# Two-layer state-space and gated-scan network with routed experts: step-width products moved from VectorE to GpSimd, and the second router's rows turned back by TensorE instead of rebuilt by GpSimd

## What is computed

```python
# layer 0, attention part: a selective state-space model, 256 inner channels, 16 states
dt = softplus(einsum('blr,dr->bld', dt, W_dt) + b_dt)        # the step width
A_bar = exp(dt[..., None] * A)
Bu = dt[..., None] * Bm[:, :, None, :] * xc[..., None]       # step width * input * B
_, h_all = associative_scan(comb, (A_bar, Bu), axis=1)
y = einsum('bldn,bln->bld', h_all, Cm) + D_param * xc
...
# layer 1, expert part: h is the modulated layer norm, routed to 2 of 16 experts
h = _layernorm(x, axis=-1) * (1 + cb) + sb
x = x + gb * _L1_ffn_ref(h, ...)                             # scores from h, experts on h
```

## Time and profile before

| what | value |
|---|---|
| runs without profile, median of 3 | 703.18 us (699.43 to 703.41) |
| the profiled execution, span | 766.7 us; no other time of it is recorded |
| VectorE (DVE) busy | 503.8 us (66%) |
| GpSimd (POOL) busy | 438.7 us (57%) |
| TensorE (PE) busy | 525.1 us (68%), mean granted clock 0.816 |
| ScalarE (ACT) busy | 334.2 us (44%) |
| state-space stage, first bu to last GpSimd product | 48.90 to 303.94, 255.0 us |

### The profile page before, as it was taken

One profiled execution on the slowest core, in us unless ns is written; L12 is line 12 of the kernel. 1 busy time (PEld: TensorE's weight loads), 2 busy tenths in 40 slices (PEclk: granted clock), 3 DMA queues, 4 the chain that ended last, 5 costly groups with the idle time before them and its releaser, 6 DMA issues.

```text
span 766.7 us, 8988 instructions
## 1 busy us (share of the span) xinstructions
PE 525.1 (68%) x2044; PEld 326.2 (43%) x2045; DVE 503.8 (66%) x909; ACT 334.2 (44%) x644; POOL 438.7 (57%) x331
## 2 busy tenths in 40 slices
PE   4568949987998889456767791678147777566630
PEld 2223314423433334356657791236125555355530
DVE  5958898899799899741422244448852667754526
ACT  3265834645575453112222245646013777970004
POOL 0047968986898998145655644307236663067650
PEclk9878979997998799657987896668557999799775
DMA  5043424332323420125656764000101112211115
GB/s 170 0 154 97 125 101 154 123 125 73 107 100 109 135 86 22 37 84 147 186 156 180 192 180 124 0 0 17 39 18 45 41 38 24 110 41 44 38 45 160
DMA packets 45292, 69.56 MB, mean 91 GB/s; under 512 B 6146, under 2 KB 25188, under 8 KB 45124
## 3 DMA queue, kind: packets, MB, share of 16 engines
q1 hardware_dynamic: 39684, 57.69, 24.3%
q0 software_dynamic: 5568, 11.41, 5.6%
HBM read 59.97 MB, written 9.11 MB: 90 GB/s over the span
## 4 chain that ended last, share of the span: by engine, by line
PE 47%; DVE 17%; issue 12%; ACT 7%; another core or an unknown queue 6%; DMA 4%; POOL 3%; DVEq 2%; SPq 1%; ACTq 0%; POOLq 0%
PE ps L1021 11%; PE ps L1144 5%; PE ps L1133 4%; PE ps L988 4%; PE ps L1293 4%; DVE hs L1575 4%; PE ps L1015 3%; PE ps L1257 2%; PE ps L1183 2%; PE ps L1282 2%; POOL bu L474 2%; PE ps L958 1%; DVEq L1644 1%; PE ps L1262 1%
## 5 line engine op out<-in xcount | busy, mean ns | idle before, releaser
L474 POOL TENSOR_TENSOR bu<-uT,b_sb 128x1024 f32<-128x1024 f32 x64 | 149.5, 2356 | 29.7 <-DVE uT L1555 29.7
L444 POOL DMA_INDIRECT y_dram<-ys,rows_i x87 | 89.6, 1030 | 93.1 <-DVE ys L1832 39.5
L438 POOL DMA_INDIRECT xl<-h_dram,rows_i x87 | 90.4, 1039 | 75.6 <-DVE rows_i L1478 41.7
L1021 PE MATMUL ps<-prod,cst 128*128 128x512 f32 x256 | 129.7, 651 | 2.9 <-DVE yT L1595 2.9
L647 ACT ACTIVATE ps<-dtT,neg_a 128x512 f32<-128x512 f32 x128 | 85.6, 685 | 64.1 <-DVE hs L1575 63.6
L485 POOL TENSOR_TENSOR prod<-hs,c_sb 128x1024 f32<-128x1024 f32 x32 | 75.6, 2363 | 31.7 <-DVE hs L1575 17.6
L1021 PEld LDWEIGHTS ps<-prod,cst 128*128 128x128 f32 x256 | 50.1, 206 | 82.1 <-issue 77.6
L1575 DVE TENSOR_TENSOR_SCAN hs<-ps,carry,bu 128x512 f32<-128x512 f32 x64 | 77.6, 1265 | 5.1 <-ACT ps L647 5.1
L1575 DVE TENSOR_TENSOR_SCAN hs<-ps,bu 128x512 f32<-128x512 f32 x64 | 73.8, 1205 | 4.6 <-ACT ps L647 4.5
L1144 PE MATMUL ps<-w_s,ht 128*128 x312 | 50.2, 312 | 27.3 <-ACT ht L737 14.4
L737 ACT ACTIVATE ht<-ps,b1T 128x128 f32<-128x128 f32 x78 | 24.8, 365 | 86.8 <-remote 40.3
(11 more groups left out here) (252 smaller groups left out, 940.3 us busy)
## 6 DMA issues: line engine op xcount, KB each, us to landing
b_sb<-b_rows SPq DMA_DIRECT2D x32, 512.0 KB, 4.5
w1r<-in_w SPq DMA_DIRECT2D x39, 256.0 KB
c_sb<-b_rows SPq DMA_DIRECT2D x32, 256.0 KB, 3.6
mf_s<-in_mf SPq DMA_DIRECT2D x16, 256.0 KB
w_s<-in_w SPq DMA_DIRECT2D x9, 256.0 KB, 4.0
h_dram<-h_tok SPq DMA_DIRECT2D x8, 256.0 KB
phase_s<-in_phase SPq DMA_DIRECT2D x16, 128.0 KB
down_s<-in_down SPq DMA_DIRECT2D x1, 2048.0 KB, 7.3
```

What stands on the lines that cost most here:

```text
L438: pool.indirect_dma_start(xl[:, j % slots, :], None, h_dram[l], bass.IndirectOffsetOnAxis(ap=rows_i[:, 0, j:j + 1], axis=0)).then_inc(load ...
L444: pool.indirect_dma_start(y_dram[l], bass.IndirectOffsetOnAxis(ap=rows_i[:, 1, j:j + 1], axis=0), ys[:, j % XR, :], None).then_inc(saved[j ...
L474: nc.gpsimd.tensor_tensor(bu[:, g % RING, :, :], uT[:, c % 2, :, :], b_sb[:, k % BRING, g % 2, :].unsqueeze(1).broadcast_to([P, ND, CHUNK] ...
L1021: last = nc.tensor.matmul(bank(Y_BANK + d), ident, prod[:, g % RING, d, :], start=n == 0, stop=n == NS - 1)
```

## The change

1. In the state-space stage VectorE keeps the sum of the step width, which now counts up a new semaphore dt_sum. The product uT stays on VectorE for chunk 0 only; for chunks 1 to 3 GpSimd makes it in `step_inputs`, two instructions of 128x512 behind products(2k-1) of the last pair of the chunk before. dt_ready is now for GpSimd's `inputs` alone; all others wait for dt_sum.
2. In the second layer GpSimd's four `router_rows` are gone. TensorE turns hT back (`turn_home`, 4 transposes a chunk into PSUM bank HOME), and ScalarE copies the block into h_tok (`rows_home`, 128x512) and counts up rows1.

```diff
+HOME = PG
...
-            def router_rows(l, c, turned, count, done):
+            def router_rows(c):
...
+            def step_inputs(c, d):
+
+                q = c % 2
+                pool.wait_ge(S["dt_sum"], 2 * c + d + 1)
+                nc.gpsimd.tensor_tensor(uT[:, q, d, :], dtT[:, q, d, :], xcT[:, q, d, :], ALU.mult).then_inc(S["dt_ready"], 1)
+
             for k in range(PAIRS):
                 inputs(2 * k)
                 inputs(2 * k + 1)
                 if k:
                     products(2 * k - 1)
+                if k % (NS // 2) == NS // 2 - 1 and k + 1 < PAIRS:
+                    for d in range(ND):
+                        step_inputs(k // (NS // 2) + 1, d)
...
             inverse_std(1, "ln2", "rs2")
-            router_rows(1, 0, "t2_ps", 1, "rows1")
             inverse_std(2, "ln2", "rs2")
             inverse_std(3, "ln2", "rs2")
-            router_rows(1, 1, "t2_ps", 2, "rows1")
-            router_rows(1, 2, "t2_ps", 3, "rows1")
-            router_rows(1, 3, "t2_ps", 4, "rows1")
...
+            def rows_home(c):
+
+                act.wait_ge(S["home_ps"], c + 1)
+                nc.scalar.activation(h_tok[:, c * CT:(c + 1) * CT, :].rearrange("p t c -> p (t c)"), bank(HOME), ACT.Copy).then_inc(S["rows1"], 1)
...
             columns_router(1)
+            rows_home(0)
             normed_out(2)
             columns_router(2)
+            rows_home(1)
             normed_out(3)
             columns_router(3)
+            rows_home(2)
+            rows_home(3)
...
+            def turn_home(c):
+
+                pe.wait_ge(S["hT2"], c + 1)
+                if c:
+                    pe.wait_ge(S["rows1"], c)
+                h = chunk_of(hT, c)
+                for t in range(CT):
+                    last = nc.tensor.transpose(ps[:, HOME, t * P:(t + 1) * P], h[:, t * P:(t + 1) * P], ident)
+                last.then_inc(S["home_ps"], 1)
...
                 dve.wait_ge(S["softp_done"], 2 * c + d + 1)
-                then(nc.vector.tensor_tensor(dtT[:, q, d, :], dtT[:, q, d, :], bank(dt_bank(d)), ALU.add))
-                nc.vector.tensor_tensor(uT[:, q, d, :], dtT[:, q, d, :], xcT[:, q, d, :], ALU.mult).then_inc(S["dt_ready"], 1)
+                nc.vector.tensor_tensor(dtT[:, q, d, :], dtT[:, q, d, :], bank(dt_bank(d)), ALU.add).then_inc(S["dt_sum"], 1)
+                if c == 0:
+                    dve.wait_ge(S["dt_sum"], d + 1)
+                    nc.vector.tensor_tensor(uT[:, q, d, :], dtT[:, q, d, :], xcT[:, q, d, :], ALU.mult).then_inc(S["dt_ready"], 1)
```

More of the change, by code:

```diff
@@ L304, in adaln_two_layers @@
  "consts_b ln_stats ln_rstd h_ready hT_ps hT_sb conv_ps z_ps xc_ready zs_ready dbl_ps dtlow_sb "
- "dt_ps dt_taken softp_done dt_ready bcf_ready b_rows_saved z_raw xc_raw c_ps a_ready bu_ready scan_done prod_ready prod_pool "
+ "dt_ps dt_taken softp_done dt_sum dt_ready bcf_ready b_rows_saved z_raw xc_raw c_ps a_ready bu_ready scan_done prod_ready prod_pool "
  "sum_done y_ready o_ps x_added logit_ps logit_sb neg_ready pad_zeroed "
@@ L487, in products @@
                                         ALU.mult).then_inc(S["prod_pool"], 1)
-            def router_rows(l, c, turned, count, done):
+            def router_rows(c):
                 h = h_tok[:, c * CT:(c + 1) * CT, :]
-                wide = lambda k: mod[:, l, c // 2, k, :].unsqueeze(1).broadcast_to([P, CT, C])
-                pool.wait_ge(S[turned], count)
+                wide = lambda k: mod[:, 0, c // 2, k, :].unsqueeze(1).broadcast_to([P, CT, C])
+                pool.wait_ge(S["hT_ps"], NCHUNK + c + 1)
                 then(nc.gpsimd.tensor_tensor(h, h, wide(CB), ALU.mult))
-                nc.gpsimd.tensor_tensor(h, h, wide(SB), ALU.add).then_inc(S[done], 1)
+                nc.gpsimd.tensor_tensor(h, h, wide(SB), ALU.add).then_inc(S["h_ready"], 1)
+            def step_inputs(c, d):
+                q = c % 2
+                pool.wait_ge(S["dt_sum"], 2 * c + d + 1)
+                nc.gpsimd.tensor_tensor(uT[:, q, d, :], dtT[:, q, d, :], xcT[:, q, d, :], ALU.mult).then_inc(S["dt_ready"], 1)
             for k in range(PAIRS):
@@ L501, in _ @@
                     products(2 * k - 1)
+                if k % (NS // 2) == NS // 2 - 1 and k + 1 < PAIRS:
+                    for d in range(ND):
+                        step_inputs(k // (NS // 2) + 1, d)
             products(STEPS - 1)
-            router_rows(0, NCHUNK - 1, "hT_ps", 2 * NCHUNK, "h_ready")
+            router_rows(NCHUNK - 1)
             rows_known(0)
@@ L628, in dt_parts @@
                 if c:
-                    act.wait_ge(S["dt_ready"], 2 * c)
+                    act.wait_ge(S["dt_sum"], 2 * c)
                 nc.scalar.activation(dtT[:, c % 2, d, :], bank(b), ACT.Relu, bias=b_dt[:, d:d + 1])
@@ L642, in decays @@
                 if n == 0:
-                    act.wait_ge(S["dt_ready"], 2 * c + 2)
+                    act.wait_ge(S["dt_sum"], 2 * c + 2)
                 for d in range(ND):
@@ L972, in z_half @@
                 if d == 0 or c == 0:
-                    pe.wait_ge(S["dt_ready"], 2 * c + d + 1)
+                    pe.wait_ge(S["dt_sum"], 2 * c + d + 1)
                 else:
@@ L1030, in project_out @@
                 if c + 1 < NCHUNK:
-                    pe.wait_ge(S["dt_ready"], 2 * c + 4)
+                    pe.wait_ge(S["dt_sum"], 2 * c + 4)
                 if c and c + 1 < NCHUNK:
@@ L1043, in rows_back @@
                 if c + 2 < NCHUNK:
-                    pe.wait_ge(S["dt_ready"], 2 * c + 6)
+                    pe.wait_ge(S["dt_sum"], 2 * c + 6)
                 if c + 1 == NCHUNK:
@@ L1233, in _ @@
             rows_router(1)
+            turn_home(0)
             score_second(1)
             rows_router(2)
+            turn_home(1)
             score_second(2)
             rows_router(3)
+            turn_home(2)
             score_second(3)
+            turn_home(3)
             ranks(1, E1)
```

## The result

The changed kernel takes 707.26 us (median of 20 executions, 703.59 to 711.55) against 703.40 us for the kernel before on the same chip (20 executions): ratio 1.0049, 95% interval 1.0031 to 1.0067. The forecast was 688.3 us and the range 680 to 700, so it lies outside. On a second chip the same pair gave 1.001 (0.9981 to 1.0038). A ratio leaves out executions more than 1.5% above the fastest of their kernel; a median is over all of them.

What follows compares the result with a forecast made beforehand. GpSimd was taken to set the state-space stage's pace, with VectorE's chain bounding the second router. The stage's -9.7 us and the router's -5.2 us made -14.9 us, so 703.2 became 688.3 us; range 680 to 700 us.

Steps and rivals of the forecast that it cites:

- The 6.48 and 6.73 us of idle GpSimd go: State-space stage, ends of chunks 0 and 1: GpSimd's idle time behind VectorE's two locked-out uT products disappears, -13.2 us.
- the tiny operations: State-space stage: small VectorE operations such as the 128x4 one get in beside GpSimd each time, 1.07 us at most; nothing charged.
- Six products on GpSimd: State-space stage: six 128x512 uT products added on GpSimd at 1.27 us each, all charged, +7.6 us.
- The stretches: State-space stage: two GpSimd instructions lengthened by 0.44 us each beside VectorE's uT no longer are, -0.9 us.
- Idle time that thins out: State-space stage: a third of the remaining 14.1 us of GpSimd's idle time goes, -4.7 us.
- Router rows that get in at the next boundary: VectorE's step 15, chunks 1 and 2: each waits some 0.7 us for a running GpSimd instruction to end, +1.5 us.
- Rival 2: Lockouts multiply: three at 6.6 us each, over router rows and ln_nmr products, give 706.6 us, slower; chance 0.06.
- Second router: Second layer's router: without GpSimd's row operations VectorE is no longer blocked, so its chain shortens, -5.2 us.
- The stage forecast: The state-space stage of the changed kernel would take near 245 us, against 255.0 in the first profile.
- what would show it: Expected signs: six GpSimd uT of about 1.27 us, no long idle there, stage near 245 us, second router's mask_b earlier.
- the first sign of being wrong: State-space stage: a VectorE operation with two SBUF inputs taking over 5 us would show the prediction wrong.
- rival 3: GpSimd bounds the stage and removed idle time returns at another wait, 705.6 us; or lockouts belong to one execution; chance 0.12.

Runs made afterwards that it cites:

- before_again: The kernel before, unchanged, run again for a second profile: 743.32 us, ratio 1.0012 of the kernel before on the same chip.
- after_ln_pointer: The changed kernel with VectorE's 128x4 product ln_nmr written as four 128x1 products with a per-partition scalar: 737.27 us, ratio 0.9863 of the kernel before.
- no_two_input: Kernel before plus the second-router change, uT read from PSUM, ln_nmr by per-partition scalar, VectorE's router rows of chunks 0 to 2 left out: 732.70 us, ratio 0.9706.
- part 2 alone: The kernel before with only the second-router change, uT staying on VectorE: 738.20 us, ratio 0.9933 of the kernel before.
- before_third: The kernel before, unchanged, one execution run for a third profile: 708.83 us.
- before_fourth: The kernel before, unchanged, one execution run for a fourth profile: 757.11 us.

## Why the prediction was wrong, point by point

The step that failed is "The 6.48 and 6.73 us of idle GpSimd go (-13.2)". It took two lockouts of one profiled execution as part of the kernel's time. Four profiles of the kernel before have 2, 0, 1 and 0 lockouts, with stages of 255.0, 240.6, 247.3 and 242.1 us: each is worth some 6 to 7 us of the stage. The second failure is a term put at nothing, the tiny operations: the changed kernel has a lockout of its own, on ln_nmr, +9.3 us. The terms of the sum, with before_again as the kernel before, the changed kernel, and after_ln_pointer as the changed kernel without its lockout:

- Six products on GpSimd, +7.6: measured 7.5. Right, though the bound "between 7.6 and 8.1" contradicts its own reason: six halves of 1.18 us are 7.1.
- Two lockouts, -13.2: nothing in an execution without them. Wrong.
- The stretches, -0.9: GpSimd's product groups fall from 76.6 to 75.2 us busy, -1.4 (bu stays at 150.8). About right.
- Idle time that thins out, -4.7: it falls from 15.1 to 6.8, -8.3. Undersized: without the wait behind the convolutions (4.1 and 4.4 us) it falls from 11.0 to 2.4, more than three quarters, and I charged a third.
- Router rows that get in at the next boundary, +1.5: right in kind. The sum behind the product at step 15 takes 2.72 us in both chunks (0.69 before), 4.1 us more on VectorE. GpSimd runs on meanwhile; what the stage pays for it is in the idle time above, and no run separates it.
- "Tiny operations such as the 128x4 one got in each time": wrong. ln_nmr was held for 8.45, 8.46 and 8.48 us in all three profiles that have part 1 as it stands, +9.3 with what follows. Rival 2 had this mechanism and gave 706.6 us. That this is close to the measured time is luck: it needed three lockouts, and one was enough, since the 13.2 us weren't there to be gained.
- Second router, -5.2: measured -0.67% alone (-0.31 to -1.03), 15.0 us to mask_b where 15.2 were forecast. Right.

Without lockouts on either side the stage goes from 240.6 to 238.3 us, since 7.5 - 1.4 - 8.3 = -2.2. With the lockout of ln_nmr it is 247.4, 6.8 us more than 240.6, where the forecast had 9.7 less. So the change is -2.3 + 9.1 - 5.2 = +1.6 us against an execution of before without a lockout; measured were 3.9 and 0.7 us. The times alone don't say how many timed executions of before carry one, and some 2 us stay open.

The stage forecast ("near 245") and most signs in "what would show it" came out nearly as written, against the wrong start: a profile 14 us too long in just the stage that was changed. But the first sign of being wrong came too, a two-SBUF-input operation of over 5 us (ln_nmr, 8.45 us). I had the doubt in rival 3 ("the lockouts belong to the profiled execution alone", 63.5 us longer than the median) and gave it 0.12 together with another case, with no sum of its own. The sentence on the Trainium skill (SBUF — State Buffer, "Who interferes with whom") deserved more weight too. Its rule, that the second to issue waits until the first finishes, came to +3.5 us for the stage, with the second router -1.7 us in all. That is nearer to the measured 3.9 and 0.7 than the forecast, though it has no lockouts, and without lockouts the stage measured -2.3. It describes what most such instructions do: in the state-space stages of the 16 profiles other than no_two_input, ln_nmr in the pointer form aside, 128 VectorE instructions with two SBUF inputs were issued into a running GpSimd instruction, and 114 got in at its end. The other 14 were held over three or four more, which the rule doesn't cover.

## What to carry to other kernels

A rare, long wait in a single profile is not a term of the sum until a second profile of the same kernel shows it; where it would pay for the whole change, work out the sum without it first. Where VectorE and GpSimd both run full, find all VectorE instructions with two SBUF tensors, the tiny ones too: in several of these kernels, moving or rewriting one left another to be held. In the changed kernel, rewriting one of 128x4 so that it reads one tensor and a per-partition scalar was worth 1.5% (0.9863 against 1.001), more than the change under study; beside part 2 alone no such gain shows.

## What the runs showed of the hardware

- A VectorE instruction with two SBUF inputs, once it has lost a boundary, waited until GpSimd ran out of work: 7.70 to 10.25 us in all 14 cases, whether it works on 128x512 or 128x4. The six of 128x512 ended 0.55 us behind GpSimd's last instruction, the eight of 128x4 0.02 us behind it. Nothing came out between 2.8 and 7.7 us.
- Where the request falls matters. At a boundary from a bu to a product that followed without a pause 13 of 51 requests were held; at the other boundaries without a pause 1 of 50 (the 10.25 us one, between two bu). The last 27 of the 128 asked ahead of a pause and got in there.
- The distance from the request to the end of the running GpSimd instruction doesn't decide it alone. Of twelve uT that asked 0.45 to 0.50 us ahead of the boundary, four were held and eight not, some at the same place of the same kernel (before_third at 154.07 held; before_fourth at 153.27 got in, both between a bu and a product). At 1.53 to 1.57 us ln_nmr was held three times of three, between a bu and a product, while uT at 1.53 to 1.56 us got in four times of four, between two bu. What decides is open.
- The form with a per-partition scalar (128x1, the second factor read as a scalar) was never held: twelve products in each stage of the six profiles that have it, all of 0.20 to 0.21 us, and all 72 asked while a GpSimd instruction ran. Nor was uT with one input in PSUM, 18 times of 18 at 0.69 us beside a running GpSimd instruction.
